# Layer 1 of a gated cross-attention kernel: Pool's subtraction in three parts, and the context's turn two slots later

## The reference

```
Q = (X @ Wq.T + bq).reshape(b, lq, h, d)
KV = (encoder_out @ Wkv.T + bkv).reshape(b, lk, h, 2 * d)
K, V = (KV[..., :d], KV[..., d:])
scores = jnp.einsum('bqhd,bkhd->bhqk', Q, K) / SCALE
weights = jax.nn.softmax(scores, axis=-1)
attn = jnp.einsum('bhqk,bkhd->bqhd', weights, V).reshape(b, lq, h * d)
out = attn @ Wo.T + bo
```

## Time and profile before

| | us |
|---|---|
| median of 3 runs (lowest, highest) | 1311.85 (1311.23, 1313.99) |
| profiled execution, its own time | 1311.5 |
| its span | 1309.6 |
| PE busy | 1133.5 (87%) |
| DVE busy | 923.1 (70%) |
| ACT busy | 716.4 (55%) |
| POOL busy | 560.2 (43%) |

### The profile page before, as it was taken

The page is one execution under the profiler, slowest core; times in us unless marked ns, Lnnn a source line. Parts: engine busy times, 40 slices in busy tenths (PEclk is TensorE's granted clock), DMA queues, the critical chain, the costliest instruction groups (busy, mean ns, idle before and its releaser), DMA issues.

```text
span 1309.6 us, 27739 instructions
## 1 busy us (share of the span) xinstructions
PE 1133.5 (87%) x10078; PEld 646.3 (49%) x10080; DVE 923.1 (70%) x1252; ACT 716.4 (55%) x983; POOL 560.2 (43%) x360
## 2 busy tenths in 40 slices
PE   0869899999999996887968899899999999999974
PEld 0335566566665655533424454544545454454542
DVE  6656666666666664777787767678686767777768
ACT  0525455555555545545666666566665656666642
POOL 5357766666666724234034323333333333333220
PEclk9979899999999999899999999999999999999996
DMA  5233334433443351000049878868677786867630
GB/s 157 71 91 82 82 97 106 119 80 101 107 112 81 83 146 38 1 21 27 1 73 141 147 154 141 161 135 156 135 148 154 139 156 136 162 135 136 119 68 14
DMA packets 256726, 137.91 MB, mean 105 GB/s; under 512 B 229184, under 2 KB 239920, under 8 KB 256672
## 3 DMA queue, kind: packets, MB, share of 16 engines
q1 hardware_dynamic: 250416, 134.03, 49.1%
q10 hardware_dynamic: 6256, 3.16, 1.0%
HBM read 49.64 MB, written 0.52 MB: 38 GB/s over the span
## 4 chain that ended last, share of the span: by engine, by line
PE 55%; DVE 12%; issue 9%; DMA 7%; SPq 6%; ACT 6%; ACTq 3%; POOL 1%; DVEq 0%; another core or an unknown queue 0%; POOLq 0%
PE bank L854 9%; PE bank L872 8%; PE bank L718 7%; PE bank L742 6%; DMA region<-u_w 5%; PE bank L746 5%; PE bank L759 4%; SPq L452 4%; PE bank L820 3%; DMA region<-wg_sb 3%; ACTq L384 3%; DVE region L1713 2%; DVE e_row L1522 2%; DVE neg_max L1561 2%; ACT region L1205 2%
## 5 line engine op out<-in xcount | busy, mean ns | idle before, releaser
L1522 DVE CUSTOM_DVE_ANT_0 e_row<-bank,region 112x1500 f32<-112x1500 f32 x128 | 220.1, 1720 | 125.4 <-PE bank L718 124.1
L1561 DVE TENSOR_REDUCE neg_max<-bank 128x1 f32<-128x1500 f32 x112 | 192.3, 1717 | 139.9 <-PE bank L854 139.9
L1205 ACT ACTIVATE region<-bank 125x896 f32<-125x896 f32 x192 | 176.0, 917 | 203.1 <-PE bank L746 203.0
L854 PE MATMUL bank<-region 128*128 128x500 f16 x1008 | 233.5, 377 | 3.3 <-ACT e_row L1232 1.8
L1241 ACT COPY region<-bank 128x768 f16<-128x768 f16 x224 | 178.2, 795 | 105.2 <-PE bank L820 105.2
L1232 ACT ACTIVATE e_row<-bank,neg_shift 128x1500 f32<-128x1500 f32 x112 | 169.4, 1513 | 84.5 <-DVE neg_shift L1565 84.3
L536 POOL CAST u_w<-e_row 128x1500 f16<-128x1500 f32 x56 | 81.8, 1461 | 210.9 <-ACT e_row L1232 210.9
L536 POOL CAST wg_sb<-e_row 128x1500 f16<-128x1500 f32 x56 | 82.5, 1473 | 201.4 <-ACT e_row L1232 156.5
L854 PEld LDWEIGHTS bank<-region 128*128 (+1 forms) x1008 | 96.8, 98 | 106.8 <-ACT e_row L1232 2.3
L742 PE MATMUL bank<-row_of,region 112*128 112x448 bf16 x384 | 138.1, 360 | 7.9 <-ACT region L1205 7.9
L746 PE MATMUL bank<-region 97*128 (+1 forms) x768 | 137.8, 260 | 0.0
(11 more groups left out here) (222 smaller groups left out, 1610.2 us busy)
## 6 DMA issues: line engine op xcount, KB each, us to landing
c_in<-in_ctx SPq DMA_DIRECT2D x32, 750.0 KB
region<-region SPq DMA_DIRECT2D x64, 192.0 KB, 2.8
region<-in_mask_Bx1xSxS_if SPq DMA_DIRECT2D x32, 328.1 KB
region<-region SPq DMA_DIRECT2D x64, 96.0 KB, 2.6
region<-region SPq DMA_DIRECT2D x8, 750.0 KB
g_w<-region SPq DMA_DIRECT2D x8, 750.0 KB
x_norm_t<-inverse_rows SPq DMA_DIRECT2D x16, 256.0 KB, 3.6
x_norm_t<-inverse_rows SPq DMA_DIRECT2D x16, 192.0 KB, 3.6
```

The lines of the kernel that those rows point to most:

```text
L854: last = pe.matmul(score_banks1(par, t)[:, k, :], q1[:, ql, b, 128 * t:128 * (t + 1)], c_t1[par][:, cl, 4 * k:4 * k + 4, 0:KP], start=(ql ...
L1205: act.activation(p0[:, 2 * i:2 * i + 2, :], ring0("s", h, i)[0:KP, :, 0:HALF_ROWS], ACT.Exp, scale=SCALE0)\
L1522: dve.tensor_tensor_reduce(out=masked.rearrange("p (a k) -> p a k", a=3), in0=bank[0:R0, 0:3, 0:4 * KP], in1=mask_bias[par][:].rearrange(" ...
L1561: dve.tensor_reduce(neg_max[:, t:t + 1], score_banks1(par, t), AX.XY, ALU.max, negate=True)\
```

## The change

Pool's subtraction is cut into three, each of 4 of the 12 chunks of 128 columns, one behind the cast of each of tiles 2, 3 and 4. Its semaphore counts to 3 for each context. SP's turn of the context moves from slot 2 to slot 4, behind the turn of tile 4 and ahead of the keep copy. The first context's low half, ahead of layer 1, is made in three parts as well, one right after another.

```
@@ sync_load_context, sync_keep, sync_turn_context1: the counts
-                wait_apart(sp, "sp", (sem("split_done1"), b - 1))
+                wait_apart(sp, "sp", (sem("split_done1"), 3 * (b - 1)))
...
-            wait_apart(sp, "sp", (sem("split_done1"), b + 1))
+            wait_apart(sp, "sp", (sem("split_done1"), 3 * (b + 1)))
...
-                    if t == 2 and not last:
+                    if t == 4 and not last:
                         sync_turn_context1(sp, b + 1, 1 - par)
                     if t == GROUPS1[1][0] and not last:
                         sync_keep(sp, b + 1, 1 - par)
...
-        def pool_context1(pool, b, par):
+        def pool_context1(pool, b, par, third):
 
             pool.wait_ge(sem("high1"), b + 1)
-            pool.tensor_tensor(c_split1[0:KP, 1], c_in[par][:], c_split1[0:KP, 0], ALU.subtract)\
+            part = slice(4 * third, 4 * third + 4)
+            pool.tensor_tensor(c_split1[0:KP, 1, part], c_in[par][:, part], c_split1[0:KP, 0, part], ALU.subtract)\
                 .then_inc(sem("split_done1"), 1)
...
                     pool_high1(pool, b, par, t)
-                    if t == 2 and not last:
-                        pool_context1(pool, b + 1, 1 - par)
+                    if 2 <= t < 5 and not last:
+                        pool_context1(pool, b + 1, 1 - par, t - 2)
...
-                pe.wait_ge(sem("split_done1" if n else "high1"), 1)
+                pe.wait_ge(sem("split_done1" if n else "high1"), 3 if n else 1)
```

More of the change, by code:

```diff
@@ L661, in _ @@
             pool_rstd(pool, 1, TT, (0, TT))
-            pool_context1(pool, 0, 0)
+            for third in range(3):
+                pool_context1(pool, 0, 0, third)
             low_weights(2)
```

## The result

| us | before | after |
|---|---|---|
| median (lowest, highest) | 1312.31 (1311.23, 1313.99), 4 runs | 1369.79 (1364.55, 1372.82), 4 runs |
| span of the profiled execution | 1309.6 | 1369.2 |
| first scores of layer 1, start | 657.75 | 662.53 |
| from there to the end of the span | 651.9 | 706.7 |
| PE busy | 1133.5 | 1171.2 |

The ratio is 1.0433 [1.0397, 1.0468]: slower by 57 us, where 36 were forecast (1348, range 1333 to 1370). The median lies 0.2 us inside the upper end of the range, and the four runs lie on both sides of that end.

The account below looks back on a forecast made before the run. TensorE was taken to bound layer 1, so only its gaps could move. Eight odd batches at +1.8 us (14.4) and seven even at +3.1 (21.7) made 36; 1311.85 + 36 = 1348 us, range 1333 to 1370.

Parts of the forecast that it names:

- What bounds the kernel, and what the change removes: Layer 1 is TensorE's; only gaps can move: 1.54 us in slot 3, 0.48 in slot 5, DMA gaps 12.1 in all.
- The additions of 1.9 us: VectorE's additions in batches 0 to 14 wait for Pool's subtraction; with thirds of 1.15 us the 1.83 us block goes.
- The turn's landing: In slot 4 on SP, the context is there 3.54 + 5.6 + 0.15 = 9.3 us after tile 4's low half started.
- Odd and even batches: Layer 1's batches: odd +1.8 us each, 8 counted; even +3.1 each, 7 counted, with the later load and the hold.
- no hold: Even batches: Pool's third holds VectorE's low half 1.10 us; by the skill's rule 0, and the sum would be 1340.
- Rival 2: TensorE's clock falls in slot 6's 3.8 us gaps; scores cost 2 us more at each of 15: +30, 1378; chance 0.2.
- The low halves of 2.8 us: Sign named: in even batches VectorE's low halves in slot 4 would take about 2.8 us.
- Two more Pool instructions: Ahead of layer 1: they cost 0.3 us on Pool beside other work, counted as nothing.
- The wait of slot 6: Sign named: scores wait for a DMA some 3 to 4 us in batches 0 to 14, TensorE's largest DMA wait.
- the missing DMA gap of slot 5: TensorE's wait for a low half's DMA in slot 5, 0.48 us in batch 5, would be gone.
- The load is later against slot 6: Even batches: keep copy, row address copies and load on SP all come 1.0 us later against TensorE.

Follow-up runs that it names:

- turn_slot3: Kernel before with the context's turn one slot later, in slot 3, Pool's subtraction whole: 1301.38 us, ratio 0.9930.
- split_only: Kernel before with Pool's subtraction in three parts back to back in slot 2, the turn still in slot 2: 1306.77 us, ratio 0.9957.
- turn_only: Kernel before with only the context's turn moved to slot 4, Pool's subtraction whole in slot 2: 1378.70 us, ratio 1.0508.
- thirds_turn_first: Changed kernel with the context's turn in slot 4 ahead of the turn of tile 4 instead of behind it: 1318.39 us, ratio 1.0045.
- busy_wait: Changed kernel with 16 more matmuls, results overwritten, on TensorE ahead of slot 6's wait for the context: 1356.80 us, ratio 1.0347.
- one_input: Kernel before with VectorE's addition of 128 single values using a constant in place of a second tensor: 1309.55 us, ratio 0.9983.
- after_load_later: Changed kernel with the load of the context after the next in slot 1 instead of at the batch's head: 1373.53 us, ratio 1.0472.
- halves_slot3: Changed kernel with the subtraction in two halves, behind the casts of tiles 2 and 3, and the turn in slot 3: 1321.28 us, ratio 1.0064.

## Why the prediction was right or wrong

The mechanism that was forecast explains 36 to 40 of the 57 us; the rest is a term that the sum did not have. That the time still came out inside the range, by 0.2 us, is luck as much as foresight.

**What bounds the kernel, and what the change removes.** Right. The additions of 1.9 us and the value products' DMA waits went, and a third took 1.15. turn_slot3 and split_only show the two gains apart, 10 and 6 us.

**The turn's landing.** Right, and the center of the loss. Issue 3.54 after the low half of tile 4, landing 5.6, release 0.15 made 9.3; measured is 904.52 − 895.13 = 9.39. The gap in slot 6 was put at 3.8 us and is 3.73 to 3.79 in most batches. That turn_only has the same gaps and thirds_turn_first hardly any shows its cause.

**Odd and even batches, with the clock kept.** Right in size, as busy_wait shows, where the clock is kept in slot 6. Its slot 6 starts at 859.43, 900.24, 940.45, 981.23 and 1020.25. Odd batches take 40.8 where 39.2 stood before: +1.6, forecast +1.8. Even ones take 40.2 and 39.0 instead of 36.2 and 35.8: +4.0 and +3.2, forecast +3.1; the first of the two holds a stretch at the slow clock, from 929.85. From layer 1 on it is +39.6, forecast 36. The Trainium skill's page "Advanced Engine Details and Errata" (Mode Summary), by whose list of modes no hold would be, would have made that 28. The forecast read that section alone: the same page, under "GPSIMD Details", names VectorE instructions with two inputs in SBUF as in conflict with Pool too. The runs agree: split_only and one_input show that a subtraction or addition of two tensors in SBUF is held, by 1.0 us in the former and 1.8 in the latter.

**TensorE's clock: the step that failed.** The sum had no term for it. Rival 2 described it, named the gap of 3.8 us, and priced it at 2 us in each of 15 places, 1378 in all; it was given 0.2. All that stood against it was the full clock of the pair in the earlier trace rows, whose longest gap was 1.6 us. No row of before showed a gap of 3.8 at full clock, and the earlier trace rows showed 0.83 where TensorE was mostly idle. The mechanism came true in 14 of 15 places. "TensorE: Matmul & The Clock Gate" of the Trainium skill (HAM oscillation), which warns of bursts between waits, is borne out by 0.50 in 904.50:908.00.

Its size: gross 31.3 us of busy time from layer 1 on, 2.1 for each gap; the transposes and value products behind the scores are slow too. Rival 2 had priced 30 and added them to the time in full. Net, filling the gaps gives back 13 by the medians of busy_wait and the changed kernel, 15 in the profiled executions; all slow stretches together may cost more, since the clock fell in busy_wait as well. The difference is the even batches' chain: with TensorE late, the turn behind the load is there almost in time (a wait of 0.86 at 926.38 instead of up to 4.0), and the addition of slot 4 is held for 0.4 instead of 1.0. The low halves of 2.8 us that the prediction named for slot 4 came in neither kernel (the longest are 1.92 and 2.19): the addition ahead of them took the hold.

**The sum again.** 36 forecast; +3.6 that busy_wait shows beyond it, the slow stretches that it still has included; +15.2 that its filling gives back: 54.8 from layer 1 on. The last 4.8 us to the spans' 59.6 lie ahead of layer 1: its first scores start at 662.53, not 657.75. Two more Pool instructions there were costed at nothing. Of the seven kernels with three parts six start at 660.8 to 662.5, those with one or two parts at 657.8 to 660.4; but after_load_later, whose instructions ahead of layer 1 are the changed kernel's, starts at 657.31, so these do not cost it of themselves. What differs with it is the clock. This is 500:560 before, in the changed kernel and in after_load_later:

```profile
500.00:560.00 60.00, 44.51 (x382) 31.27 (x373) 38.91 (x67) 32.06 (x57) 26.61 (x16) 0.86 0.08 21
500.00:560.00 60.00, 46.90 (x398) 34.25 (x396) 35.28 (x62) 30.86 (x54) 24.72 (x17) 0.77 0.08 21
500.00:560.00 60.00, 44.57 (x375) 31.18 (x364) 39.12 (x68) 31.85 (x57) 26.91 (x18) 0.86 0.08 21
```

The changed kernel's granted clock is 0.77 there instead of 0.86. Why it fell for longer in this execution, and whether three parts make that likelier, stays open.

**What the prediction had asked for.** The wait of slot 6, its being the largest on DMA, the missing long additions and the missing DMA gap of slot 5 all came. The load is later against slot 6, by 915.22 − 904.52 − (890.32 − 880.72) = 1.1 (forecast 1.0). Only the long low halves did not; long additions stood in their place.

## What to carry to other kernels

When a transfer is moved later, count from its issue to its landing (here 5.7 us) against the slot of whoever needs it, and count its place in the queue too: two DMAs of one slot in the other order were worth 51 us. Price a new wait of several microseconds on TensorE above its length when the work behind it would run at the lower clock, and find out what it gives back by putting work in the gap. Removing a stall pays only if the next late thing is moved with it: the load's place was worth 24 to 27 us in two kernels, 2 to 4 in a third, and nothing where the context's turn was late.

## What the runs showed of the hardware that was not expected

- The first turn behind the 750 KB load on SP's queue releases its waiter 10.9 to 11.2 us after the load's issue, whether it was issued 2.0 (thirds_turn_first), 2.3 (halves_slot3) or 5.7 us (the changed kernel: 915.22, 920.96, 926.38) behind it. Issuing it earlier only made the issue longer (4.92, 4.50, 1.87).
- SP is held behind the copy of both halves too: the turn at 903.71 takes 7.54 us to issue, where 1.44 is usual.
- VectorE waits out the Pool instruction that is running, not Pool's queue (1.16 between parts of 1.15), and the addition with one input was not held at all (0.15).
- Slow scores came behind 14 of 15 gaps of 3.1 to 5.1 us in the changed kernel, 13 of 15 in turn_only and 15 of 15 in after_load_later. The clock also fell behind gaps of 2.05 to 3.17 us in busy_wait, while the one of 3.74 that ends at 986.72 left it at full speed.
